# Dealing fifteen counting steps of VectorE to the one-hot chunks of a routed feed-forward kernel

## The reference

```
sg = xf @ shared_gate_w.T;  su = xf @ shared_up_w.T
shared_out = silu(sg) * su @ shared_down_w.T
topk_idx, w = route(xf)           # 4 experts of 16 per token, from 2 groups of 4
g = einsum('sc,ech->esh', xf, gate_w);  u = einsum('sc,ech->esh', xf, up_w)
hw = silu(g) * u * combine.T[:, :, None]
out = x + shared_out + einsum('esh,ehc->sc', hw, down_w)
```

## Time and profile before

| what | us |
|---|---|
| median of 3 runs | 1008.75 (1003.91 to 1011.58) |
| profiled execution, its own time | 1011.18 |
| its span | 1009.4 |
| PE busy | 996.7 (99%) |
| DVE busy | 655.6 (65%) |
| POOL busy | 475.1 (47%) |
| ACT busy | 380.2 (38%) |

### The profile page before, as it was taken

The page is one execution under the profiler, slowest core; times in us unless marked ns, Lnnn a source line. Parts: engine busy times, 40 slices in busy tenths (PEclk is TensorE's granted clock), DMA queues, the critical chain, the costliest instruction groups (busy, mean ns, idle before and its releaser), DMA issues.

```text
span 1009.4 us, 21034 instructions
## 1 busy us (share of the span) xinstructions
PE 996.7 (99%) x6750; PEld 612.0 (61%) x6750; DVE 655.6 (65%) x1506; ACT 380.2 (38%) x776; POOL 475.1 (47%) x540
## 2 busy tenths in 40 slices
PE   9999999999999999999999999999999999999998
PEld 7785664444444444557787778787777544444443
DVE  4947669876288899875454555554555376676765
ACT  3626534444354543314444444444444311111111
POOL 0723512312224476755445544545444267677662
PEclk9969799999999999999999999999999999999999
DMA  9733775868663441529889888998989579999675
GB/s 349 256 117 125 270 247 160 238 169 259 188 173 132 159 131 63 156 66 249 245 253 240 248 258 238 248 249 242 235 253 241 169 232 254 315 264 300 202 228 176
DMA packets 175483, 216.93 MB, mean 215 GB/s; under 512 B 101096, under 2 KB 112232, under 8 KB 174376
## 3 DMA queue, kind: packets, MB, share of 16 engines
q1 hardware_dynamic: 151640, 136.95, 45.9%
q0 software_dynamic: 23760, 78.79, 26.7%
HBM read 123.67 MB, written 69.22 MB: 191 GB/s over the span
## 4 chain that ended last, share of the span: by engine, by line
PE 83%; DVE 9%; issue 3%; DMA 2%; ACT 1%; POOL 1%; DVEq 0%; SPq 0%; ACTq 0%; POOLq 0%
PE bank L1067 18%; PE bank L940 14%; PE bank L1130 14%; PE bank L1091 9%; PE bank L956 7%; PE bank L1143 6%; PE bank L1050 5%; PE bank L1081 2%; PE bank L715 1%; PE bank L695 1%; PE bank L792 1%; PE bank L729 1%; DVE arena L1854 1%; PE bank L734 1%; DVE arena L1568 1%
## 5 line engine op out<-in xcount | busy, mean ns | idle before, releaser
L1067 PE MATMUL bank<-arena 128*128 x1716 | 211.4, 273 | 1.0 <-issue 0.6
L940 PE MATMUL bank<-arena 128*128 128x512 f16 x888 | 204.5, 381 | 1.7 <-DMA arena<-pt_dram 1.2
L1067 PEld LDWEIGHTS bank<-arena 128*128 128x128 f16 x1716 | 162.9, 98 | 27.0 <-issue 2.1
L2138 POOL DMA_INDIRECT arena<-y_dram,arena x128 | 135.8, 1061 | 77.4 <-issue 33.7
L2081 POOL DMA_INDIRECT arena<-xr_dram,arena x143 | 139.6, 976 | 58.1 <-issue 46.6
L940 PEld LDWEIGHTS bank<-arena 128*128 128x128 f16 x888 | 88.0, 100 | 103.0 <-DMA arena<-pt_dram 1.7
L1130 PE MATMUL bank<-arena 128*128 128x512 f16 x648 | 144.1, 379 | 0.0
L1091 PE MATMUL bank<-arena 128*128 x429 | 115.4, 378 | 0.5 <-ACT arena L1400 0.5
L1950 DVE SCALAR_TENSOR_TENSOR arena<-arena 128x512 f32<-128x512 f32 x128 | 95.4, 750 | 30.7 <-DMA arena<-y_dram,arena 25.8
L1883 DVE SCALAR_TENSOR_TENSOR arena<-bank,arena 128x128 f32<-128x128 f32 x143 | 41.7, 292 | 108.9 <-ACT arena L1389 79.4
L1337 ACT ACTIVATE arena<-arena 128x512 f16<-128x512 f32 x64 | 40.3, 630 | 185.7 <-DVE arena L1615 107.9
(11 more groups left out here) (227 smaller groups left out, 1340.1 us busy)
## 6 DMA issues: line engine op xcount, KB each, us to landing
y_dram<-arena SPq DMA_DIRECT2D x143, 256.0 KB
arena<-in_x SPq DMA_DIRECT2D x8, 1024.0 KB, 12.1
xr_dram<-arena SPq DMA_DIRECT2D x16, 512.0 KB, 4.0
x_dram<-arena SPq DMA_DIRECT2D x8, 1024.0 KB, 5.7
arena<-in_gu_w SPq DMA_DIRECT2D x16, 512.0 KB, 3.5
out<-arena SPq DMA_DIRECT2D x32, 256.0 KB
arena<-x_dram SPq DMA_DIRECT2D x5, 1024.0 KB, 6.0
arena<-in_gu_w POOLq DMA_DIRECT2D x8, 512.0 KB, 4.3
```

What stands on the lines that cost most here:

```text
L940: last = mm(bank[half][:, :], (gu_hi_s, gu_lo_s)[wp][:, c, at:at + H], xt[:, xv * KC + kc, :], start=(n == 0), stop=(n == 3 * KC - 1))
L1067: last = mm(gate_up_bank(s, s)[:, 0:2 * H], rows[:, xv * KC + kc, :], only((gu_hi_r, gu_lo_r)[wp], e, slice(kc * 2 * H, (kc + 1) * 2 * H)) ...
L2138: pool.indirect_dma_start(out=ybuf[n % RING][:, e, :], out_offset=None, in_=y_dram[:, :], in_offset=bass.IndirectOffsetOnAxis(ap=row_of[:, ...
```

## The change

The 15 counting steps with the zeroing ahead of them and the cast behind them leave their place between the token table and chunk 36. A function `count_blocks` issues them in pairs, each pair behind the one-hots of a chunk: pair n behind those of the n-th chunk of `HOT`, so experts 0 and 1 behind chunk 26's, up to expert 14 with the cast and `s_expert` behind chunk 33's. Chunk 34 gets none. The tile `counted` moves to an address that no one-hot uses. Nothing is added and nothing left out.

```diff
--- before.py
+++ after.py
@@ -198,7 +198,7 @@
         before_tile, so_far_b = view(o2, [(T + 1) * E], F16), view(o2 + 6 * KB, [T * E], F16)
         so_far = before_tile[:, E:]
         xg = view(o2, [4, 2 * D], F16)
-        counted = view(o1 + 8 * KB, [COLUMNS])
+        counted = view(o1 + 9 * KB + 128, [COLUMNS])
         router_rows = view(o2 + 8 * KB, [2 * KC, BLK], F16)
         x1b = view(o2 + 16 * KB, [TB, D])
 
@@ -1855,21 +1855,27 @@
                                            token_id[:, t:t + 1], ALU.is_equal, ALU.mult)
                 last.then_inc(s_hot, 1)
 
+            def count_blocks(experts):
+
+                for e in experts:
+                    if e == 0:
+                        link.done(V.memset(counted, 0.0))
+                    link.done(V.scalar_tensor_tensor(counted, cr_sb[:, R_BLK:R_BLK + COLUMNS], last_blk[:, e:e + 1],
+                                                     counted, ALU.is_ge, ALU.add))
+                    if e == E - 2:
+                        link.start(V.memset(blocks_e[:, COLUMNS:COLUMNS + 8], 0))
+                        link.done(V.tensor_copy(blocks_e[:, 0:COLUMNS], counted))
+                        V.engine_nop().then_inc(s_expert, 1)
+
             one_hots(0)
-            for g, of_chunk in HOT.items():
+            for n, (g, of_chunk) in enumerate(HOT.items()):
                 chunk(g)
                 for t in range(max(of_chunk[0], 1), of_chunk[1]):
                     one_hots(t)
+                count_blocks(range(2 * n, min(2 * n + 2, E - 1)))
             chunk(AHEAD - 2)
             dve.wait_ge(s_hot_used, T)
             V.tensor_scalar(token_of, bank[6][:, 0:COLUMNS], ID_MID, None, ALU.add).then_inc(s_tok, 1)
-            link.done(V.memset(counted, 0.0))
-            for e in range(E - 1):
-                link.done(V.scalar_tensor_tensor(counted, cr_sb[:, R_BLK:R_BLK + COLUMNS], last_blk[:, e:e + 1],
-                                                 counted, ALU.is_ge, ALU.add))
-            link.start(V.memset(blocks_e[:, COLUMNS:COLUMNS + 8], 0))
-            link.done(V.tensor_copy(blocks_e[:, 0:COLUMNS], counted))
-            V.engine_nop().then_inc(s_expert, 1)
             chunk(AHEAD - 1)
```

## The result

| what | before | changed kernel |
|---|---|---|
| median of 13 runs each, us | 1003.91 (997.07 to 1012.91) | 1015.16 (1007.07 to 1019.84) |
| ratio, 95% interval | | 1.0108 (1.0078 to 1.0138) |
| the same, on two other occasions | | 1.0021 (0.9990 to 1.0052), 1.0100 (1.0065 to 1.0135) |
| profiled execution: time, span | 1011.18, 1009.4 | 1007.33, 1005.5 |

The account below looks back on a forecast made before the run. VectorE was taken as full up to the token table: +5.31 of counting and +2.0 of hold move it 7.3 us; with gathers 0.5 faster, `turn_rows(1)` starts +6.8 later. 1008.75 + 6.8 = 1015.6 us, range 1009 to 1020.5.

Parts of the forecast that it names:

- VectorE is full up to the token table, with 1.41 us to spare: From chunk 27 to the token table VectorE's only usable gap is 1.41 us, ahead of L1615 at 406.35.
- Counting moved ahead, +6.72: Zeroing, 15 steps and cast now stand between one-hots ahead of the token table: +6.72 − 1.41 = +5.31 us.
- The rival by which each step waits for GpSimd: Counting steps meeting GpSimd's one-hots wait; 15 at 0.65 us add 9.7 us on VectorE: 1025.3 us, chance 0.05.
- A new hold by GpSimd in chunk 31, +2.4, less 0.43: GpSimd's L2047 and L2048 hold VectorE's late one-hots in chunk 31: +2.0 us net, ends −0.4 and +2.4.
- Gathers go out faster without the counting beside them, −0.5: Behind the token table, GpSimd's copies and gathers go out faster: −0.5 us, ends 0 and −0.8.
- The transpose of block 3 shares the transfer engines, 0 to 1.3, taken as 0: SyncE's transpose of block 3 starts earlier and shares transfer engines with block 1's gathers: 0 to 1.3 us, taken as 0.
- The 1.22 us from `turn_rows(1)` to `gate_up(0)`: At the routed part's start, the way from 444.75 to 445.97 stays 1.22 us, `s_expert` being set long before.
- Stalls of TensorE in `tokens`: TensorE stands for one-hots in chunks 28, 29 and from 31 on, 6 to 8 us together.
- The signs: Token table at 443.5 to 445, counting steps of 0.37 to 0.40 us, first `gate_up` at 452 to 453, among others.
- one chance in nine for a measurement over 1%: With the runs' scatter, the forecast of +6.8 us might read over 1% slower; slower in all 0.14, the same 0.85.
- TensorE's granted clock is 1.00, so no term comes from it: In both stretches from 364.33 to 435.49 us the granted clock is 1.00, so it adds nothing to the sum.
- The hidden counting: Rival: VectorE has some 7 us of gaps ahead of the token table; 1008.2 us, faster, chance 0.10.

Follow-up runs that it names:

- second profile: The changed kernel run again unaltered, against the kernel before: ratio 1.0021 (0.9990 to 1.0052), at the same clock +6.9 ± 1.2 us.
- the kernel with steps in the waits: Against the kernel before, counting steps 0 to 7 in VectorE's 0.7 us waits of chunks 28 to 35, 7 behind the token table: ratio 1.0037.
- third profile: The changed kernel run once more unaltered, against the kernel before: ratio 1.0100 (1.0065 to 1.0135), at the same clock +7.7 ± 1.2 us.
- the lump: Against the kernel before, all 15 counting steps with zeroing and cast in one piece just ahead of the token table: ratio 1.0148 (1.0091 to 1.0205).
- the kernel with filled waits: Against the kernel before, row one-hots in VectorE's waits of chunks 26 to 34, counting in those of 24, 25, 35 and behind the table: ratios 1.0017, 1.0006.

## Why the prediction came out

*VectorE is full up to the token table, with 1.41 us to spare: right.* The gap is gone after, and doubling the steps moved the table by nearly their whole length again (5.7 of 5.9 us).

*Counting moved ahead, +6.72: it is 6.94.* A pair takes 0.76 to 0.86 us, the eight places sum to 6.94 with the zeroing and the cast. The rival by which each step waits for GpSimd (0.65 us a step) is excluded: the longest of the 15 steps took 0.46 us, 0.09 more than the plain 0.37, though GpSimd's one-hots run beside the steps in seven of the eight places. Here the measurement differs from the rule of the Trainium skill that the prediction cites, by which the later of two such instructions is blocked.

*A new hold by GpSimd in chunk 31, +2.4, less 0.43: right.* Chunk 31's part of VectorE went from 5.99 to 8.65 us, +2.66, and chunk 32's got 0.60 shorter. The Trainium skill, "SBUF — State Buffer", section "Who interferes with whom", says that VectorE in a two-port mode, which `tensor_scalar` can enter, contends with GpSimd, and that the one issued later is fully blocked. The longer rows, 2.71 and 1.61 us of L1854, agree with that; no row shows in which mode L1854 runs. Small shifts of holds in chunks 27, 29, 30, 33 and 34 add 0.2. Together 6.94 + 2.66 − 1.41 − 0.60 + 0.2 = 7.8 us: the table moved by 7.7 to 7.9, predicted 7.3.

*Gathers go out faster without the counting beside them, −0.5: it is −0.37* (3.79 to 3.42 us).

*The transpose of block 3 shares the transfer engines, 0 to 1.3, taken as 0: mis-sized.* From the start of row 1's gather to TensorE's start on the rows it takes 4.27 us in the second profile (443.53 to 447.80) and 4.22 in the kernel without counting, where the transpose is early too, against at most 3.68 before: +0.6. In the kernel with steps in the waits the gathers are spaced as before (1.62 and 1.41 us against 1.61 and 1.41), the transpose is early, and it is 4.17: so it isn't the closer spacing. Table, issue and landing make 7.8 − 0.4 + 0.6 = +8.0 where I had +6.8, and the profiles show +7.7 to +8.3 at the first `gate_up`. The 1.22 us from `turn_rows(1)` to `gate_up(0)`, taken as unchanged, are 0.98 in the second profile. In the first and third profile the gather is not the last gate: TensorE itself is, since its chunk 36 is slowed. That the fit's +7.2 ± 0.7 is less than +8.0 may come from what the clock's fall takes up in the fit and from the late wait's scatter; no run separates them.

*Stalls of TensorE in `tokens`: right in place* (chunks 28, 29 and 32 to 35, with 0.2 us in chunk 31), 7.0 to 7.2 us where 6 to 8 was said.

*The signs.* Laid on the first profile of before (365.17 plus the distance), the table is at 444.7 to 444.9, within the 443.5 to 445 that was given. The counting steps take 0.35 to 0.46 us and not 0.37 to 0.40, and the first `gate_up` lies at 453.7 to 454.2 and not at 452 to 453: it missed its sign. The prediction gave one chance in nine for a measurement over 1%; two of three occasions read 1.0 and 1.1%.

*"TensorE's granted clock is 1.00, so no term comes from it": wrong, and missing among the rivals.* It holds for before. But the change makes TensorE stand, and in all three profiles the clock then falls to half for about 3 us. What it adds beyond the gather's own wait is 0.3 to 0.5 us where it lies in chunk 36. In the second profile it came behind the gather, and the way from the first `gate_up` to the turn of block 4's rows took 11.2 us instead of 9.7: 1.5 us.

*The hidden counting: excluded* by the kernel without any counting, −0.5 ± 1.1 us.

## What to carry to other kernels

A step on the critical chain is worth moving only if the next gate behind it opens clearly earlier; here, by the prediction's estimate, a gather opened 0.05 us before it, and taking the counting out altogether won nothing. Before moving work between other work, subtract an engine's busy time from the length of that very stretch, and account for what is missing wait by wait: the mean over the whole run said 65%, the stretch had 1.4 us. Look also at what an engine escapes by little: one-hots that ended 0.13 us ahead of a GpSimd step were held for 2.7 us once they came later. Where runs scatter by the clock, compare distances inside the trace from a mark that both kernels share, and times only at the same clock.

## What the runs showed of the hardware

- Behind TensorE's stalls the granted clock went to 0.50 for some 3 us: after nine of 0.4 to 1.0 us in 78 us in the changed kernel (three profiles of three). In the lump it fell while TensorE stood for 6.17 us in one piece. With most of the short stalls filled by idle matmuls it did not fall (two of two). In the one profile of the kernel with doubled steps it stayed at 1.00 through this stretch, for which I have no reason.
- From the start of a row gather to TensorE's start on its rows it took at most 3.68 us in the three profiles of before, and 4.1 to 4.4 us in nine profiles of other kernels, where SyncE's transposing transfer began 0.4 to 0.7 us behind the gather's start.
- A two-operand GpSimd step (2.13 us) held VectorE's f16 one-hots for most of its length each time they met; and so it held counting steps (two took 2.00 us instead of 0.77 in the kernel with filled waits). Beside GpSimd's one-hots a counting step took at most 0.09 us more.
